# A Mamba layer with a mixture of experts on one core: the last chunk's second half of channels scanned in two halves of 256 tokens

## The reference

```
xn = rmsnorm(layernorm(x)) * rms_w
xs, res = split(xn @ W_in)                        # 512 channels each
xs = silu(causal_conv4(xs) + conv_b)
dt, B, C = split(xs @ W_x)                        # 512, 16, 16
dt = softplus(dt @ W_dt);  A = -exp(A_log)        # A: 512 channels x 16 states
for t: h = exp(A*dt[t]) * h + dt[t]*B[t]*xs[t];  y[t] = sum over states of h*C[t]
x1 = x + layernorm(x) + (y * silu(res)) @ W_out
xe = layernorm(x1), 512 tokens for each expert e
out = x1 + (silu(xe @ w1[e]) * (xe @ w3[e])) @ w2[e]     # 256 -> 704 -> 256
```

## Time and profile before

| | us |
|---|---|
| median of 3 runs | 983.43 (983.17 to 984.2) |
| the profiled execution | 983.61 |
| its span, from the first to the last instruction | 981.8 |
| busy: TensorE, VectorE, GpSimd, ScalarE | 915.7, 899.1, 891.0, 733.2 |
| first and last scan of the last chunk | start 831.52, end 938.96 |

### The profile page before, as it was taken

How to read it: one execution, slowest core, us unless ns; L and a number is a source line. 1 busy time by engine, 2 the same in 40 slices (tenths; PEclk the granted TensorE clock), 3 DMA queues, 4 the chain that set the end, 5 groups by cost and what they waited for, 6 DMA issues and landing times.

```text
span 981.8 us, 13018 instructions
## 1 busy us (share of the span) xinstructions
PE 915.7 (93%) x4172; PEld 598.0 (61%) x4172; DVE 899.1 (92%) x966; ACT 733.2 (75%) x1305; POOL 891.0 (91%) x425
## 2 busy tenths in 40 slices
PE   6989989999999999999999999999999997869898
PEld 4555455655766566755756557755766566745765
DVE  5889899899999999999999999999999989999951
ACT  4577877988779878888779888888779785567630
POOL 1498899999999999999999999999999999999920
PEclk9998999999999999999999999999999999679899
DMA  5580144012742049021561038220480027200110
GB/s 175 212 308 22 43 185 204 4 65 65 268 186 67 2 148 353 18 68 59 212 247 43 25 103 326 89 68 21 176 320 16 31 99 284 92 21 4 59 50 21
DMA packets 43476, 116.82 MB, mean 119 GB/s; under 512 B 8592, under 2 KB 27024, under 8 KB 34192
## 3 DMA queue, kind: packets, MB, share of 16 engines
q1 hardware_dynamic: 41552, 115.94, 32.0%
q10 hardware_dynamic: 1856, 0.04, 0.1%
HBM read 110.21 MB, written 5.77 MB: 118 GB/s over the span
## 4 chain that ended last, share of the span: by engine, by line
PE 44%; DVE 20%; issue 14%; ACT 11%; POOL 10%; DMA 1%; DVEq 0%; POOLq 0%; SPq 0%; ACTq 0%
PE gbank L1095 18%; DVE ring L658 13%; PE gbank L1109 12%; PE ybank L1158 9%; POOL hc L516 7%; DVE ring L643 4%; ACT ebank L787 2%; POOL ring L502 2%; ACT hb L1022 2%; ACT sres L872 1%; DVE hb L738 1%; PE gbank L1103 1%; ACT L1027 1%; ACT L1020 1%; DMA hb<-in_L_attn_W_x_dram 1%
## 5 line engine op out<-in xcount | busy, mean ns | idle before, releaser
L658 DVE TENSOR_TENSOR_SCAN ring<-ebank,state,ring 128x512 f32<-128x512 f32 x512 | 623.2, 1268 | 31.1 <-ACT ebank L787 24.1
L516 POOL TENSOR_TENSOR hc<-ring,c_all 128x1024 f32<-128x1024 f32 x255 | 598.5, 2368 | 12.8 <-PE ybank L1158 6.9
L787 ACT ACTIVATE ebank<-dt_,a_neg 128x512 f32<-128x512 f32 x512 | 348.0, 688 | 149.6 <-DVE ring L658 145.8
L1158 PEld LDWEIGHTS ybank<-ident,hc 128*128 128x128 f32 x2048 | 239.1, 144 | 107.3 <-issue 54.9
L1158 PE MATMUL ybank<-ident,hc 128*128 128x128 f32 x2048 | 266.0, 279 | 33.2 <-POOL hc L516 19.2
L502 POOL TENSOR_TENSOR ring<-b_all,u 128x1024 f32<-128x1024 f32 x109 | 258.1, 2368 | 9.9 <-DVE taken L607 9.5
L643 DVE TENSOR_TENSOR ring<-b_all,ubank 128x1024 f32<-128x1024 f32 x145 | 173.5, 1196 | 0.0
L1095 PE MATMUL gbank<-xT,w 128*128 128x512 f32 x320 | 147.9, 597 | 9.8 <-DVE hb L738 8.5
L1095 PE MATMUL gbank<-xT,w_a 128*128 128x512 f32 x256 | 119.7, 604 | 8.0 <-DVE dt_ L632 4.4
L1095 PEld LDWEIGHTS gbank<-xT,w 128*128 128x128 f32 x320 | 57.3, 190 | 76.5 <-issue 56.7
L1095 PE MATMUL gbank<-xs,w_a 128*128 128x512 f32 x224 | 100.8, 593 | 0.7 <-ACT sres L805 0.7
(11 more groups left out here) (146 smaller groups left out, 749.4 us busy)
## 6 DMA issues: line engine op xcount, KB each, us to landing
b_all<-bc_kept SPq DMA_DIRECT2D x32, 1024.0 KB, 6.6
c_all<-bc_kept SPq DMA_DIRECT2D x32, 1024.0 KB, 8.4
w<-in_L_ffn_w_dram SPq DMA_DIRECT2D x16, 640.0 KB, 4.9
w_a<-in_L_attn_W_in_dram SPq DMA_DIRECT2D x7, 1024.0 KB, 5.0
w_a<-wc_kept SPq DMA_DIRECT2D x7, 1024.0 KB, 4.9
w2s<-in_L_ffn_w_dram SPq DMA_DIRECT2D x8, 640.0 KB, 9.3
xin<-in_L_attn_x_dram SPq DMA_DIRECT2D x9, 512.0 KB, 3.6
x<-in_L_attn_x_dram SPq DMA_DIRECT2D x7, 512.0 KB, 6.5
```

The source lines that it names most:

```text
L516: ch_ok.by(e.tensor_tensor(hc[:, q % HC, :, :], ring[:, q % RING, :, :], c_all[:, n:n + NG, :], ALU.mult))
L658: h_ok.by(e.tensor_tensor_scan(row, ebank[j % 2][:, :], row, initial=state[:, q, n:n + 1], op0=ALU.mult, op1=ALU.add))
L787: e_ok.by(e.activation(ebank[j % 2][:, :], dt_[:, d, :], ACT.Exp, scale=a_neg[:, d, k:k + 1]))
L1158: last = e.matmul(ybank[:, cols(b)], hc[:, q % HC, n, cols(b)], ident[:, :], is_transpose=True, start=(k == 0 and n == 0 and b == 0), stop ...
```

## The change

Only the last chunk is rewritten. Its tiles 0 to 15 (d 0 and 1) stay as they are; tiles 16 to 31 become four states by 256 tokens: 16 to 19 are d 2 and 20 to 23 are d 3 for the first 256 tokens, 24 to 27 and 28 to 31 the same for the second 256. So B times u, C and the sum over states keep their sizes per tile, while scans and exponentials of these tiles are twice as many and half as long; ScalarE fills a bank with two exponentials, and VectorE waits for both. y, gate, projection, statistics, norm, transposes, gate and up are made for 256 tokens each (jobs YH, OXH, GT, UH); those of the first half stand between tiles 23 and 31, those of the second half behind the last tile. The back of chunk 6 comes some tiles earlier in this chunk. The second norm's scales are computed on ScalarE there (`scaled2`), not on GpSimd. A tuple of its own for the last chunk gives GpSimd B times u of 15 tiles, not 14: tiles 8, 16, 19, 20, 25 and 26 go to GpSimd, tiles 17, 18, 22, 24 and 27 to VectorE. TensorE sums tiles two steps behind from tile 24 on. The six matmuls that keep TensorE busy are gone.

```diff
+    POOL_BU_E = (1, 4, 7, 8, 10, 11, 14, 16, 19, 20, 21, 23, 25, 26, 29)
+    QH = Q // 2
+    HF = TC // 2
+    SN = 2 * NG
+    LAG_E = 2
+    SWITCH = 24
...
-        PLAN += [(22, "ahead", "M", 0, 40.6), (27, "ahead y", "YT", 2, 30.0), (31, "ahead", "M", 1, 40.7)]
+        FINAL = [
+            (3, "back", "YT", 3, 4.4), (4, "back", "M", 0, 8.9), (4, "back", "M", 1, 8.7), (10, "back", "OXT", 0, 10.9),
...
+        def spot(c, q):
+            if halved(c, q):
+                m = q - QH
+                return ND // 2 + m // (N // SN) % 2, m % (N // SN) * SN, SN, slice(m // GPD * HF, (m // GPD + 1) * HF)
+            return q // GPD, q % GPD * NG, NG, slice(0, TC)
+        def e_of(c, j):
+            if c < E - 1 or j < NG * QH:
+                return ebank[j % 2][:, :]
+            return ebank[j // 2 % 2][:, j % 2 * HF:(j % 2 + 1) * HF]
...
-                    e_ok.wait(e, c, j + 1)
-                    row = ring[:, q % RING, n, :]
-                    h_ok.by(e.tensor_tensor_scan(row, ebank[j % 2][:, :], row, initial=state[:, q, n:n + 1],
+                    e_ok.wait(e, c, j + 2 - j % 2 if halved(c, q) else j + 1)
+                    row = tile_of(ring, c, q)[:, n, :]
+                    h_ok.by(e.tensor_tensor_scan(row, e_of(c, j), row, initial=all_states[:, first:first + 1],
...
+                if (c, q) == (E - 1, QH):
+                    bu(c, q + 1)
+                    bu(c, q + 2)
...
-                    h_ok.wait(e, c, j - 1)
+                    h_ok.wait(e, c, j - 1 if not halved(c, q) or j == NG * QH else j - j % 2 - 2)
+                    e_ok.by(e.activation(e_of(c, j), dt_[:, d, tok], ACT.Exp, scale=a_neg[:, d, n0 + n:n0 + n + 1]))
...
+            final = [(2, "back", y_read(ND - 1)), (4, "back", residual(0, 1)), (8, "back", rooted2), (8, "back", m_copy), (8, "back", scaled2), (9, "back", normal2),
...
+                     (15, "back", gate(4)), (15, "back", tails), (16, "back", gate_silus), (16, "scan", y_read(1)), (19, "back", down_on(0)),
...
+            def ahead_normal(c, i):
+                rooted_half(0)
+                e.wait_ge(s_rth[0], 3)
+                for b in range(2):
+                    e.activation(st2[:, 3, b:b + 1], st2[:, 2, b:b + 1], ACT.Copy, scale=st2[:, 1, b:b + 1]).then_inc(s_sch[0], 1)
...
+            def expand_half(name, j):
+                def job(c, i):
+                    h, k0 = j // 3, j % 3
+                    w13_in.wait(e, c)
+                    wait_read(e, i, "OXH", h)
+                    bank = wait_free(e, i, name, j)
+                    blocks = [w13[:, :, int(name == "UH"), cols(f)] for f in range(2 * k0, min(2 * k0 + 2, FT))]
+                    if name == "GT" and k0 == 2:
+                        blocks.append(w13t[:, :, :])
+                    for n, w in enumerate(blocks):
+                        for k in range(KD):
+                            last = e.matmul(bank[:, n * HF:(n + 1) * HF], w[:, k, :], xT[:, k, h * HF:(h + 1) * HF],
+                                            start=(n == 0 and k == 0), stop=(k == KD - 1), skip_group_check=True)
+                    filled(last, i, name, j)
+                return job
```

More of the change, by code:

```diff
@@ L333, in run @@
                         group(i, q)
-                    for at, part, job in (table0 if i == 0 else last if i == E else table):
+                    for at, part, job in (table0 if i == 0 else last if i == E else final if i == E - 1 else table):
                         if at == q and on[part][0]:
@@ L648, in group @@
                     wait_bu(e, c, q)
-                st_ok.wait(e, c - 1, q // 2 + 1)
-                for n in range(NG):
-                    j = q * NG + n
+                d, n0, many, tok = spot(c, q)
+                if tok.start == 0:
+                    st_ok.wait(e, c - 1, (d * N + n0) // (2 * NG) + 1)
+                else:
+                    st_ok.wait(e, c, (q - GPD) // 2 + 1)
+                for n in range(many):
+                    j = scans(c, q) + n
                     if c == 0 and q == 0:
@@ L968, in turned_last, with scaled2, rooted_half @@
-            def turned_last(c, i):
-                move("OXT", 0, i, xT[:, 0, :])
+            def scaled2(c, i):
+                roots2.wait(e, c)
+                for b in range(NT):
+                    last = e.activation(st2[:, 3, b:b + 1], st2[:, 2, b:b + 1], ACT.Copy, scale=st2[:, 1, b:b + 1])
+                scales2.by(last)
+            def rooted_half(h):
+                two, done = slice(2 * h, 2 * h + 2), s_rth[h]
+                e.wait_ge(s_sth[h], 1)
+                e.activation(st2[:, 0, two], mv2[:, two, 1], ACT.Ln, bias=consts[:, 0, 0:1]).then_inc(done, 1)
+                e.activation(st2[:, 2, two], mv2[:, two, 0], ACT.Copy, scale=-1.0).then_inc(done, 1)
+                e.wait_ge(done, 1)
+                e.activation(st2[:, 1, two], st2[:, 0, two], ACT.Exp, scale=-0.5).then_inc(done, 1)
@@ L1087, in _ @@
                       (31, "next", turned("XT"))]
-            run(table, table0, last, group)
+            run(table, table0, final, last, group)
         @block.tensor
@@ new lines, in job, with project_part @@
+                    if ND - 1 in ks:
+                        filled(last, i, "M", t)
+                return job
+            def project_part(t, *ks):
+                def job(c, i):
+                    e.wait_ge(s_wout_in, 16)
+                    x1a_ok.wait(e, c, 2 * t + 2)
+                    bank = gbank[PLACE[i, "M", t][0]]
+                    for k in ks:
+                        if k < ND // 2:
+                            wait_read(e, c, "YT", k)
+                        else:
+                            wait_read(e, i, "YH", 2 * t + k - ND // 2)
+                        for b in range(2):
+                            last = e.matmul(bank[:, b * D:(b + 1) * D], sres[c % 2][:, k, cols(2 * t + b)], wout[:, k, :],
+                                            start=False, stop=(k == ND - 1), skip_group_check=True)
+                    if ND - 1 in ks:
+                        filled(last, i, "M", t)
+                return job
```

437 lines of the change are left out of this document (275 added, 162 removed).

## The result

The changed kernel takes 977.48 us (median of 4 runs, 977.22 to 979.27), the kernel before on the same chip 983.82 (983.17 to 984.33). The ratio is 0.9943, 95% interval 0.9931 to 0.9955: faster by 4.4 to 6.8 us. The forecast was 978.7, and "faster by over 0.2%" held 0.75 of the chance.

The account below looks back on a forecast made before the run. Last chunk: a scan phase bound by VectorE and GpSimd, then a 42.84 us tail bound by TensorE. +9.2 and -13.9 give -4.7, span 977.1; with 1.8 over the span 978.9, predicted 978.7 us, range 972.0 to 985.0.

Parts of the forecast that it names:

- 1, the tail: Behind chunk 7's last scan: only 256 tokens are left, so the tail takes 28.95 us against 42.84, -13.9.
- half clock behind the last scan: Sign of being wrong: TensorE at half clock after chunk 7's last scan, which would lengthen the tail; no size given.
- 2, the first half: Last chunk up to tile 16: GpSimd takes B times u of tiles 8 and 16; tile 16 starts at 885.5, +1.2.
- 3, scans of 256: Last chunk's second half: 64 scans of 256 at 0.65 replace 32 of 512, +3.8 us (0 to +8.3).
- the upper bound: Cost of a lone scan of 256 on VectorE, 0.72 us, with a fixed 0.17 read from products of 512 and 256.
- 4, the second half: Tiles 16 to 31: VectorE's 57.8 us of work plus waits, 3.0 of them at tile 17; last scan ends 948.2, +9.2.
- the 0.4 for ScalarE's side work at tiles 20 and 22: Added to the last scan's end because these tiles have no B times u beside ScalarE's side work: 0.4 us.
- The first down rows of chunk 6: TensorE's clock may fall at 897 to 903, delaying VectorE 1.5 at tile 24, covered by the wait at tile 26.
- GpSimd alone: Rival, last chunk: VectorE keeps up and GpSimd's sum sets the last scan at 941.9; 972.6 us, chance 0.22.
- the slower rival: Halved tiles: exponentials of 256 become the bound if over about 0.56; up to +9.6, 988.5 us, chance 0.10.
- Eaten: Rival: scans at 0.72 (+4.5) in the scan phase use up the tail's gain; 983.4 us, no change, chance 0.14.

## Why the prediction was right

Predicted from the first scan on: +9.2 for the scan phase and -13.9 for the tail, -4.7 together. Measured: +8.7 and -13.4, -4.70. Both terms are 0.5 too large, and the errors cancel: that the sums agree so closely is luck. The forecast of 978.7 lies 1.2 over the median of the runs, and that part no traced execution explains.

*1, the tail.* 28.95 predicted, 29.43 found: y sum to 3.36 behind the last scan (3.0 predicted), 8.68 of short steps (8.7), gate and up 9.50 (9.5), two down rows 5.19 (5.2), the end 2.70 (2.55). By TensorE's timeline the list from the y sum of tile 27 on ran without a gap, from 937.97 to 951.43: 13.46, where 13.3 were counted, and it began 10.1 ahead of the end of the last scan, where 10.3 were taken. What the step did not see is that the two rows also keep the clock: it priced them at their own length, and the experiments show that leaving them at the end would have cost 2.7 us on top by the clock. The prediction named half clock behind the last scan as what would make it wrong; the changed kernel has 0.99 there.

*2, the first half.* Tile 16 starts at 885.66, counted from the first scan 53.74 behind it; predicted 885.5, 53.98. VectorE waits 2.84 at tiles 10 and 11, 2.6 predicted. The norm's steps were hidden, as costed. But that the scales moved to ScalarE was no detail: with the normalisation moved up to tile 9, GpSimd's list would have held it up, and the scans by 6, had the scales stayed behind tile 8 there; behind tile 6 they cost 0.17. The prediction weighed the edit by its instructions alone (0.5 on ScalarE, where they took 0.84, and 0.23 on GpSimd), and no step of it asked what the queue would have cost.

*3, scans of 256.* Eight of them in a row take 5.24: a pitch of (5.24 - 0.73) / 7 = 0.644, 0.65 predicted; at this pitch the term is +3.5 instead of +3.8. A scan by itself takes 0.727 on average; the upper bound, from products of 512 and 256, was 0.72. By the rule of the Trainium skill (VectorE: DVE Perf Modes, section on the trn2 errata) each of the 32 more instructions would have cost an estimated 0.157, 5.0 together. The trace comes near it for a scan by itself, 2 x 0.727 - 1.268 = 0.19 (the prediction's 0.17 for it was read from products, not from scans), and has less for scans in a row, 2 x 0.644 - 1.18 = 0.11. The measurement decides, and with it the estimate of 1.2 us more falls.

*4, the second half.* The wait at tile 17 was to be 3.0 with the copy of y as its cause: it is 3.26, and two experiments that take the cause away from either end remove 2.56 and 1.91 of it. One link was smaller than told: the y sum is late because TensorE's list has no gap up to it, and the fourth up block's wait for its bank, which the prediction gave as the reason, adds only 0.2 (the third and fourth take 3.63 up to the start of the sum; two up blocks without such a wait take 3.43 in the kernel with the up block later). GpSimd was to go on at 898.0 and to end B times u of tile 26 at 925.9: 898.51 and 926.34, 0.5 and 0.4 late, where the first scan was 0.4 late. From there to the end of the last scan 22.3 were counted and 21.7 came. The term that failed is the 0.4 for ScalarE's side work at tiles 20 and 22: VectorE shows no wait there, and these tiles lie ahead of tile 26, whose start GpSimd sets. That is most of the 0.5 in the scan phase. The first down rows of chunk 6 might fall into half clock and would then cost 1.5 at tile 24, hidden by the wait of 1.5 at tile 26. TensorE's timeline of the first two:

```profile
903.76 7.94 PE L1262 MATMUL gbank<-w2s,hb 128*128 128x256 f32 x24 [1.76 <-ACT gbank L1145]
```

And TensorE in a stretch of 2 us there (busy time, granted clock 0.50):

```profile
904.00:906.00 2.00, 2.00 (x5) 0.50 0.03 8
```

So 24 instructions took 7.94, not 5.2. The wait at tile 24 is 1.64 and the one ahead of tile 26 only 0.32, and where an edit took the wait at tile 24 away (B times u of 17 and 18 back) tile 26 came no earlier: GpSimd ended its B times u 95.0 behind the first scan, 94.4 in the changed kernel. Where a part of the wait at tile 17 went first, the wait at tile 24 was 0.7 to 0.8 and free as well.

*The rivals.* "GpSimd alone" had the right engine for the stretch from tile 17 to tile 26, but it left out GpSimd's gap. When the copy of y is moved and GpSimd relieved of two pieces, the time reaches 974.28, near the 972.6 worked out there, but not by that rival's path: there VectorE is the one that hardly waits (0.9), and GpSimd waits for it. Exponentials of 256 take 0.468 (two in 0.87), under the 0.56 from which the slower rival decides. Its round rests on a misread row: 903.24 is the end of the first of two exponentials, not of the second, which ends at 903.84; the 0.12 from an exponential's end to the scan stands. "Eaten" needed scans at a pitch of 0.72, and it is 0.644.

## What to carry to other kernels

Where two engines feed each other, find the one whose list sets the pace of the stretch, and add up only its own idle time: waits of the other cost nothing until they make a gap there (3.73 to 1.14 in GpSimd's gap was 2.54 in the scans). A hand-over of 0.2 us to an engine with a full list can cost the time of what stands ahead of it (here 8.2 of waiting and 6.2 in the scans), so place it by the backlog or leave the small work where its consumer is. Work moved into a gap may also keep TensorE's clock up (2.7 us here): ask of each gap that a move opens or closes what the products behind it run at.

## What the runs showed that was not expected

- The last product of the ring with C on VectorE (128x512) took 0.69 in the changed kernel, at the end of GpSimd's own (from 946.87, 1.27); before, it took 1.33, from 938.99, beside GpSimd's. What sets the difference was not tried.
- The first scan of the last chunk started between 829.78 and 832.55 in the twelve profiled executions, though nothing ahead of it differs. The clock record differs early: TensorE waits 4.4 us for VectorE at about 68 to 73 and then has a mean granted clock of 0.66 between 70 and 80 in eight of them and 0.83 in four; the four start that scan at 829.78 to 830.69, the eight at 830.68 to 832.55. What decides between the two was not found. Counting from the first scan of the stretch under study takes it out.
